# A two-layer decoder on one core: the context's conversion moved to GpSimd in halves, the odd heads' low parts to VectorE

## The reference, cut to what matters

```python
def _L0_xattn_ref(query, bank, Wq, bq, Wk, bk, Wv, bv, Wo, bo):
    q = split_heads(query @ Wq + bq)
    k = split_heads(bank @ Wk + bk)
    v = split_heads(bank @ Wv + bv)
    scores = jnp.einsum('bhqd,bhkd->bhqk', q, k) / scale
    attn = jax.nn.softmax(scores, axis=-1)
    out = jnp.einsum('bhqk,bhkd->bhqd', attn, v)
    ...
    return out @ Wo + bo
...
x = _layernorm(x + _L0_attn_ref(x, ...), axis=-1)
x = _layernorm(x + _L0_xattn_ref(x, ctx_1024, ...), axis=-1)
x = _layernorm(x + _L0_ffn_ref(x, ...), axis=-1)
x = _layernorm(x + _L1_attn_ref(x, ...), axis=-1)
x = _layernorm(x + _L1_xattn_ref(x, ctx_1024, mask_BxS2_ik0, ...), axis=-1)
x = _layernorm(x + _L1_ffn_ref(x, ...), axis=-1)
```

## Time and profile before

| | |
|---|---|
| median of 3 runs | 2411.67 us (2410.17 to 2414.68) |
| the profiled execution, its own time | 2410.11 us |
| its span, first to last instruction | 2408.3 us |
| mean granted clock of PE | 0.927 |
| busy: PE, PEld | 2155.8, 1981.5 us |
| busy: DVE, ACT, POOL | 1076.1, 961.1, 784.4 us |
| chain that ended last, by engine | PE 75%, DVE 9%, POOL 7%, issue 4%, ACT 4% |

### The profile page before, as it was taken

How to read it: one execution, slowest core, us unless ns; L and a number is a source line. 1 busy time by engine, 2 the same in 40 slices (tenths; PEclk the granted TensorE clock), 3 DMA queues, 4 the chain that set the end, 5 groups by cost and what they waited for, 6 DMA issues and landing times.

```text
span 2408.3 us, 36414 instructions
## 1 busy us (share of the span) xinstructions
PE 2155.8 (90%) x12528; PEld 1981.5 (82%) x12528; DVE 1076.1 (45%) x1728; ACT 961.1 (40%) x1623; POOL 784.4 (33%) x576
## 2 busy tenths in 40 slices
PE   4699999999765889689999999969999999999997
PEld 3688888888654778578888888869999999999987
DVE  8465666556456278435555666555510003000032
ACT  2255655455442244334555555442222223111132
POOL 4433332233333633422333323222222222222234
PEclk9799999999777978789999999979999999999999
DMA  4355455445321100254554545311112111111123
GB/s 152 119 136 141 131 143 152 117 131 139 106 65 31 38 8 0 80 176 126 136 141 133 143 133 156 110 54 61 61 62 61 61 53 61 61 61 61 61 70 98
DMA packets 127576, 230.56 MB, mean 96 GB/s; under 512 B 40024, under 2 KB 77144, under 8 KB 127384
## 3 DMA queue, kind: packets, MB, share of 16 engines
q1 hardware_dynamic: 127512, 229.71, 33.2%
HBM read 174.12 MB, written 55.53 MB: 95 GB/s over the span
## 4 chain that ended last, share of the span: by engine, by line
PE 75%; DVE 9%; POOL 7%; issue 4%; ACT 4%; DMA 1%; SPq 1%; POOLq 0%; DVEq 0%; ACTq 0%
PE psS L310 13%; PE psS L312 13%; PE psS L311 13%; PE psO L1638 5%; PE psJ L310 4%; PE psJ L311 4%; PE psJ L312 4%; PE psS L1595 3%; POOL cT_lo L511 3%; PE psT L310 2%; PE psT L311 2%; PE psT L312 2%; PE psT L1624 2%; PE psS L1624 2%; DVE psS L1162 1%
## 5 line engine op out<-in xcount | busy, mean ns | idle before, releaser
L703 POOL TENSOR_TENSOR fw_lo<-raw,fw_hi 128x1024 fp32r<-128x1024 f32 x96 | 235.1, 2451 | 551.4 <-ACT fw_hi L968 551.4
L310 PE MATMUL psS<-hid_hi,fw_hi 128*128 128x400 f32 x1152 | 398.2, 346 | 3.4 <-DVE hid_lo L1521 2.9
L312 PE MATMUL psS<-hid_hi,fw_lo 128*128 128x400 f32 x1152 | 399.0, 346 | 0.0
L311 PE MATMUL psS<-hid_lo,fw_hi 128*128 128x400 f32 x1152 | 398.6, 346 | 0.0
L518 POOL TENSOR_TENSOR pT<-p,pT 128x600 fp32r<-128x600 f32 x112 | 165.2, 1475 | 644.2 <-ACT pT L788 644.2
L1162 DVE TENSOR_REDUCE psS<-psS 100x1 f32<-100x722 f32 x256 | 234.7, 917 | 194.9 <-PE psS L1595 194.2
L1521 DVE TENSOR_TENSOR hid_lo<-h_act,hid_hi 128x800 fp32r<-128x800 f32 x32 | 40.8, 1343 | 528.1 <-ACT hid_hi L1057 528.1
L310 PE MATMUL psJ<-cT_hi,wk_hi 128*128 128x362 f32 (+1 forms) x512 | 190.2, 371 | 65.7 <-POOL cT_lo L511 39.2
L310 PEld LDWEIGHTS psS<-hid_hi,fw_hi 128*128 128x128 f32 x1152 | 217.3, 189 | 7.0 <-DVE hid_lo L1521 4.7
L312 PEld LDWEIGHTS psS<-hid_hi,fw_lo 128*128 128x128 f32 x1152 | 218.7, 190 | 0.0
L311 PEld LDWEIGHTS psS<-hid_lo,fw_hi 128*128 128x128 f32 x1152 | 217.2, 189 | 0.0
(11 more groups left out here) (318 smaller groups left out, 4573.7 us busy)
## 6 DMA issues: line engine op xcount, KB each, us to landing
kS<-k_parts SPq DMA_DIRECT2D x384, 180.5 KB
raw<-ffn_dram SPq DMA_DIRECT2D x96, 512.0 KB, 3.5
k_parts<-kst SPq DMA_DIRECT2D x64, 362.0 KB, 3.2
k_parts<-kst SPq DMA_DIRECT2D x64, 360.0 KB, 2.8
ctx_raw<-ctxT_dram SPq DMA_DIRECT2D x32, 361.0 KB, 3.9
ctx_late<-ctxT_dram SPq DMA_DIRECT2D x28, 361.0 KB, 3.8
qS<-q_parts SPq DMA_DIRECT2D x192, 50.0 KB, 2.2
q_parts<-qst SPq DMA_DIRECT2D x16, 400.0 KB, 2.5
```

The costliest lines, as they stand in the source:

```text
L310: nc.tensor.matmul(out, st[0], mv_[0], start=first, stop=False)
L311: nc.tensor.matmul(out, st[0], mv_[1], start=False, stop=False)
L312: return nc.tensor.matmul(out, st[1], mv_[0], start=False, stop=last)
L703: nc.gpsimd.tensor_tensor(fw.lo[:, e, :], raw[:, e, :], fw.hi[:, e, :], ALU.subtract)\
```

## The change

Four things are changed.

- The odd heads' plain exponential stays in PSUM for all pairs (psT), ahead of it the high part is written, and DVE makes the low part, at the end of each pair. POOL's `odd_probs_lo` and the tile p are gone. PE's waits for pT's high part or for POOL become waits for `att_lo_odd`, which DVE now raises.
- The context of the next batch is converted on POOL alone, high part (a `tensor_copy`, a CAST in the program) and low part, by halves of the keys: the first half of chunks 0 and 1 at pair 2, of chunks 2 and 3 at pair 3, the second half of all four at pair 4. The first half may be written after keys(3, 0), the last reader of it, and the second after keys(3, 1). SP loads chunks 2 and 3 by halves too. The stage's first batch is converted as before.
- keys of the next batch move one pair ahead: (0, 0), (0, 1), (1, 0), (1, 1) in the pairs 4, 5, 6, 7. keys(1, 1) leave the end of the batch. Only pair 3 is without keys, and has the rows set behind the odd exponentials.
- ACT applies the norm in pair 6 and not 3, POOL adds the bias in pair 6 and not 2. SP's order follows the keys.

The diff, cut to this:

```diff
-CONTEXT_AT = {2: (0,), 3: (1,), 4: (2, 3)}
-KEYLESS = (3, 4)
+KEYLESS = 3
 KEYS_AT = {0: (2, 1), 1: (3, 0), 2: (3, 1)}
-NEXT_KEYS_AT = {5: (0, 0), 6: (0, 1), 7: (1, 0)}
+NEXT_KEYS_AT = {4: (0, 0), 5: (0, 1), 6: (1, 0), 7: (1, 1)}
...
 SP
-            def context_rest(L, b):
-
-                wait_apart(sp, A.k_mm, 2 * C * (NB * L + b))
-                for c in range(2, C):
-                    sp.dma_start(ctx_late[:, c, :], d["ctxT"][c, :, bass.ds(b * KEYS, KEYS)])\
-                      .then_inc(A.more_in, 16)
+            def context_late(L, b, i):
+
+                k0, kn = HALVES[i]
+                wait_apart(sp, A.k_mm, 2 * C * (NB * L + b - 1) + 7 + i)
+                sp.dma_start(ctx_late[:, 2:4, k0:k0 + kn],
+                             d["ctxT"][2:4, :, bass.ds(b * KEYS + k0, kn)].rearrange("c p n -> p c n"))\
+                  .then_inc((A.late_a, A.late_b)[i], 16)
...
                     keys_out(L, b, 3, 0)
+                    if not last:
+                        context_late(L, b + 1, 0)
                     keys_in(L, b, 5)
                     if not last:
                         queries_in(L, b + 1, 0)
                     keys_out(L, b, 3, 1)
                     if not last:
-                        context_rest(L, b + 1)
+                        context_late(L, b + 1, 1)
...
 POOL
-            def odd_probs_lo(L, b, t):
-
-                h = 2 * t + 1
-                wait_apart(pool, A.pt_hi, H * (b + NB * L) + h + 1)
-                nc.gpsimd.tensor_tensor(pT[:, h % 4, :, T:2 * T], p[:, t % 2, :].rearrange("p (k t) -> p k t", k=NKC),
-                                        pT[:, h % 4, :, 0:T], ALU.subtract).then_inc(A.lo_odd, 1)
+            def context_half(L, b, cs, i):
+
+                n = b - 1 + (NB - 1) * L
+                for c in cs:
+                    if c < 2:
+                        wait_apart(pool, (A.ctx_in0, A.ctx_in1)[c], 16 * (b + NB * L + 1))
+                    else:
+                        wait_apart(pool, (A.late_a, A.late_b)[i], 16 * (n + 1))
+                    if c == 0:
+                        wait_apart(pool, A.k_mm, 2 * C * (b - 1 + NB * L) + 7 + i)
+                    src, hi, _ = half_part(c, i)
+                    nc.gpsimd.tensor_copy(hi, src).then_inc(A.half_hi, 1)
+                for c in cs:
+                    wait_apart(pool, A.half_hi, 8 * n + 4 * i + c + 1)
+                    src, hi, lo = half_part(c, i)
+                    nc.gpsimd.tensor_tensor(lo, src, hi, ALU.subtract).then_inc(A.half_lo, 1)
...
                     for t in range(PAIRS):
-                        if t != 4:
-                            odd_probs_lo(L, b, t)
...
-                        if t == 2:
+                        if t in (2, 3) and not last:
+                            context_half(L, b + 1, (2 * t - 4, 2 * t - 3), 0)
+                        if t == 4 and not last:
+                            context_half(L, b + 1, range(C), 1)
+                        if t == 6:
                             add_bias(L, b, None, base + b, A.resid_done)
-                        if t in CONTEXT_AT and not last:
-                            for c in CONTEXT_AT[t]:
-                                context_lo(L, b + 1, c)
...
 ACT
-                def odd_probs(b, t, psum=False):
+                def odd_probs(b, t):
 
                     B, h = b + NB * L, 2 * t + 1
-                    dst = st_view[1] if psum else p[:, t % 2, :].rearrange("p (i n) -> p i n", i=2)
                     act.wait_ge(A.st_mm, H * B + h + 1)
-                    wait(act, A.lo_odd, PAIRS * B + t - (0 if psum else 1))
...
+                    nc.scalar.activation(pT[:, h % 4, :, 0:T].rearrange("p (i k) t -> p i k t", i=2),
+                                         st_view[1].rearrange("p i (k t) -> p i k t", k=HK), ACT.Exp, scale=SCALE)\
+                      .then_inc(A.pt_hi, 1)
+                    nc.scalar.activation(st_view[1], st_view[1], ACT.Exp, scale=SCALE).then_inc(A.exped, 1)
...
-                        if t in KEYLESS and not last:
-                            context_hi(L, b + 1, CONTEXT_AT[t][0])
-                        if t < PAIRS - 1 and t not in KEYLESS:
+                        if t < PAIRS - 1 and t != KEYLESS:
                             max_rows(b, t + 1)
-                        odd_probs(b, t, psum=t == 4)
-                        if t in KEYLESS:
+                        odd_probs(b, t)
+                        if t == KEYLESS:
                             max_rows(b, t + 1)
-                        if t == 2 and not last:
-                            context_hi(L, b + 1, 0)
-                        if t == 3 and not first:
+                        if t == 6 and not first:
                             norm_apply(b - 1)
-                        if t == 4 and not last:
-                            context_hi(L, b + 1, 3)
...
 DVE
                         if t in NEXT_KEYS_AT and not last:
                             keys_lo(L, b + 1, *NEXT_KEYS_AT[t])
+                        low_parts(b, 2 * t + 1)
                         if t == 0 and not first:
                             norm_stats(base + b - 1, 0, y[:, 0, :])
-                        if t == 4:
-                            low_parts(b, 2 * t + 1)
...
 PE
-                if g == 0 and i == 0 and not weights and 0 in cs:
-                    pe.wait_ge(A.ctx_even, 2 * B + 2)
-                    pe.wait_ge(A.ctx_odd, 2 * B + 2)
                 for c in cs:
+                    if g == 0 and not weights and c in (0, 2):
+                        pe.wait_ge(A.half_lo, 8 * (b - 1 + (NB - 1) * L) + 4 * i + c + 2)
...
                     if h % 2 == 0:
                         wait(pe, A.lo_even, PAIRS * B + h // 2)
-                    elif h == 11:
-                        pe.wait_ge(A.lo_odd, PAIRS * B + 5)
                     else:
-                        wait(pe, A.pt_hi, H * B + h - 1)
+                        wait(pe, A.lo_odd, PAIRS * B + h // 2)
...
                     weighted(b, H - 1)
                     if not last:
-                        keys(L, b + 1, 1, 1)
                         scores(b + 1, 0)
```

More of the change, by code:

```diff
@@ L433, in attention_loads @@
                 first()
-                with nc.sync.Fori(0, NB - 1) as b:
+                batch(0, False)
+                with nc.sync.Fori(1, NB - 1) as b:
                     batch(b, False)
```

73 lines of the change are left out of this document (33 added, 40 removed).

## The result

The changed kernel takes 2517.5 us (median of 4 runs, 2514.8 to 2526.8), the kernel before 2412.0 (2410.2 to 2414.7) beside it: a ratio of 1.044, 95% interval 1.042 to 1.047. The forecast had the side right and the size wrong: it said 2455, +43, and +105 came. The profiled execution has a span of 2515.5 us and a mean granted clock of 0.905 (0.927 before). One run of all that follow, 2816.2 us at a granted clock of 0.71 in experiment 10, stands apart from the others of its kernel and is left out.

A forecast was written before the change was run, and what follows sets the result against it. TensorE, busy 90% of the span, was taken as the bound. The profiled 2410.1 us plus 31.5 for fourteen batches (+2.25 each, clock term included) and 13 for the last batches made 2454.6, forecast 2455, range 2412 to 2490.

The forecast's parts named there:

- The gain side: Savings a batch: context wait of 1.88 us gone, head 9 to 11 scores −0.4, 11 to 13 −1.5, keys(1, 1) −2.0.
- S11 to S13: On PE, from the start of head 11's scores to head 13's: 6.2 us in place of 7.72, −1.5.
- the slack: On GpSimd, idle time and 4 us before the converted context is wanted, said to cover the casts and subtractions.
- The ring: DVE's odd low part awaits ACT's exponential, delaying maximum and next odd scores: pairs with keys take 6.2 us, not 5.2.
- Rival B: The ring doesn't bind: pairs stay at PE's 5.2 us, 63.45 a batch, 2325 us, faster; chance 0.12.
- rival C: The context comes late and PE waits at keys(0, 1): 2 us in each of 14 batches, 2483 us; chance 0.06.
- 1.3 × 1.7 = 2.3: Clock term a batch: 1.3 stretches at 1.2 GHz after PE's waits, each costing 1.7 us.
- two longer ones, 5: Upper end of the clock term: two longer stretches at 1.2 GHz in a batch, 5 us.
- Rival A: The clock stays up: a batch takes 69.45 us, 2422 us in all; chance 0.22.
- +0.6 on the 68.85: Sum of all interval changes in a batch at full clock, on the 68.85 us batch read before: 69.45.
- keys(1, 1) leave the end of the batch: −2.0: On PE behind head 15's scores: twelve projection matmuls go, 2.0 us less; the pair after keeps its length.
- +6.5 a stage, 13 in all: Each stage's last batch, keyless from pair 3: +1.6 for two intervals, +4.0 up to head 9's scores, −0.7 at the end.

The follow-up runs named there:

- experiment 10: The kernel before, context and keys untouched, with all odd low parts on DVE behind the next pair's even maximum and the fold of the outputs: 2458.4 us.
- experiment 7: The changed kernel, its DVE order untouched, with eleven unused 128x362 matmuls in pair 3 and eleven more in pair 1: 2456.6 us.
- Experiment 1: The changed kernel with DVE's odd low part moved behind the next even head's maximum, still ahead of the fold of the outputs: 2397.0 us.
- experiment 5: The changed kernel with DVE's odd low part moved behind both the next even head's maximum and the fold of the outputs: 2374.9 us.
- experiment 9: experiment 6 with six more unused matmuls in each of the pairs 3 to 6 of both last batches: 2344.7 us.
- experiment 11: experiment 4 with GpSimd converting the context ahead of the odd low part in pairs 2 to 4, no filler: 2333.1 us.
- experiment 4: The changed kernel with the odd heads' low parts back on GpSimd in all pairs, ahead of the context's conversion: 2480.7 us.
- experiment 6: experiment 5 with six unused 128x362 matmuls added in pair 3: 2352.8 us.
- experiment 12: experiment 11 with the unused matmuls of experiment 9: 2335.7 us.

## Why the prediction was right or wrong

**The gain side held.** The 1.88 wait for the context is gone, and S11 to S13 fell by 1.6 in experiment 7 (forecast −1.5), S9 to S11 by 0.38 (forecast −0.4). The casts (0.49) were within the bounds, the subtractions took 0.97 and not 0.87, and the slack covered both.

**The ring held.** Intervals measured without the clock's part, in experiment 7: S2 to S5 +1.6 (forecast +1.7), S5 to S7 +0.95 (+0.9), S7 to S9 +1.6 (+1.4), S13 to S15 +0.7 (+0.5). Rival B is out, and so is rival C: no wait for the context's low part is among those of stage 0. Experiment 1 is the direct proof: with the low part elsewhere 120 of the changed kernel's 2517 us go, the stretches at 1.2 GHz that hung on the ring among them.

**Three terms were mis-sized**, and they make up the 62 us between 2455 and 2517.5.

*The clock, "1.3 × 1.7 = 2.3" a batch.* This is the step that failed most. Measured: 76.03 less the 71.46 of experiment 7, both means over fourteen, 4.57 a batch, 2.27 × 14 = 32 us more. I had the number of stretches about right (1.3 a batch, and the trace has 20 in fourteen), and took the cost of one, 1.7 us, from one batch of the kernel before. In the changed kernel a stretch mostly lasts about 10 us, and such a one costs 4.1 us (75.2 against the 71.1 of experiment 7; 4.4 in experiment 5), about two and a half times what I gave it. The kernel before already had such stretches, in batches that I didn't read; here is one of four, and then the one that I read:

```profile
188.79:259.34 70.55, 66.96 (x421) 59.19 (x420) 42.07 (x71) 38.10 (x68) 21.41 (x19) 0.93 0.50 135
...
328.35:397.21 68.86, 64.27 (x422) 56.86 (x420) 42.07 (x71) 38.10 (x68) 21.43 (x19) 0.98 0.51 138
```

My upper bound, "two longer ones, 5", held it. Rival A, the clock stays up, is out; had it come, it would not have been 2422 either, but near the 2456.6 of experiment 7. The Trainium skill (TensorE: Matmul & The Clock Gate, HAM oscillation) blames, in that section, idle gaps longer than any in these batches; by it the clock term would be 0. The traces disagree: waits of 1.8 to 2.0 us at a sparse pair were followed by 1.2 GHz again and again, and filling the pairs took 61 us off (2517.5 to 2456.6).

*The ring's full clock sum, "+0.6 on the 68.85".* It was 71.1, another 1.65 × 14 = 23 us. Most of that is "keys(1, 1) leave the end of the batch: −2.0", which came as −0.7. I wrote that the pair after S15 keeps its length, and did not look at what queues behind the odd low part of pair 6. It is the fold, and `weighted` waits for it: 0.74 in the rows above. Experiments 1 and 5 show it: 16.0 with the low part ahead of the fold, 14.45 with the fold ahead. I had looked for what is queued behind the waiting instruction and found the maximum, but not the fold. The rest is 0.2 in each of two rounds, and that is the fold too. It stands behind the even maximum, ends at 388.34 (387.78 + 0.56 above), and `weighted` starts at 388.49; so from S15 to the turned maxima it takes 2.76 and not 2.48. Behind S5, where no fold is due, it took 2.53 even after a wait of 1.98.

*The last batches, "+6.5 a stage, 13 in all".* Measured +6 and +15. In stage 0 the figure is about right. In stage 1 S2 to S15 takes 42.9 us where it took 29.4, +13.5, and behind S15 it is +1.7. Up to S9 it is +4.3, as forecast (+4.0). From S9 to S15, windows of the kernel before and of the changed one:

```profile
1563.66:1576.42 12.76, 10.93 (x91) 9.38 (x91) 10.61 (x20) 8.95 (x17) 4.05 (x4) 1.00 0.43 107
```

```profile
1659.98:1681.87 21.89, 19.30 (x91) 16.76 (x91) 12.12 (x22) 8.37 (x15) 0.00 (x0) 0.50 0.22 52
```

These are three intervals, and I had counted two, +1.6 each. They took 6.4, 7.8 and 7.8 us at 1.2 GHz, where my ring had 5.9. So one interval was left out, and the clock was given no term here. Filling the last pairs gained 8 us in experiment 9, but in a kernel with another ring, so how the 9.1 us divide between ring and clock is not shown.

32 + 23 + 8 = 63 us, against 62.5. That the sum closes is no proof, since the last batches are what the fourteen left over.

**What the forecast did not see at all** is that the change was two changes of opposite sign, large ones. It summed them into "+0.6 a batch" and called the side by the clock. The side would have been right without the clock, for a reason that I had not summed so: with the gaps filled (experiment 7) the changed kernel is still 44 us slower, by the ring and the fold. The half with the context was worth −79 us by itself, close to what rival B worked out (63.45 a batch and 2325; experiment 11, with the odd low parts still on GpSimd, has 63.8 and 2333). I had tied that gain to the condition that the ring doesn't bind, and read the 12% as small; the ring did bind, but only for where one line stands, and with that line moved (experiment 5) a batch at full clock takes 64.4.

## What to carry to other kernels

Moving work to an engine with room is judged by what stands behind it in that engine's queue, and by when its input comes, before its duration is: a 0.78 us instruction that waits for late data cost 143 us more at the end of a pair than two places later, and the same fault on GpSimd (experiment 4 against 11) cost 148; both numbers hold the clock's part. For each such instruction list everything behind it that another engine waits for, not only the nearest; the fold was missed that way, in the prediction and in experiment 1. And when a change has parts that can stand alone, time them alone, each in its best place, before judging the whole.

## What the runs showed of the hardware

A short wait on TensorE can cost more than its length, by the lower clock behind it. In the changed kernel every one of the fourteen waits of about 1.8 us ahead of S9, in the pair without keys, went with a stretch at 0.50, mostly of some 10 us. Ahead of S5 the same wait of 1.98 us left the clock at 1.00 in the first of the two batches shown and was followed by such a stretch in the second. In experiment 5 waits of 0.54 and 0.59 us within 2 us stood where it began, and the same two in the batches that stayed at full clock; experiment 11 has the 0.54 there and not the 0.59, and no stretch. A stretch of 10 us costs 4.1 us in the changed kernel and 4.4 in experiment 5, so that unused matmuls in the gap pay: −40 us for 11 in pair 3, a further −21 for 11 in pair 1, −22 for six in experiment 6, −11 in the kernel before, and nothing where the clock was up already (experiment 12). In stage 0 of experiment 5 batches with equal instructions alternate between 64.4 and 68.8 us; what decides which of the two a batch becomes was not found.

On GpSimd a cast from fp32 to fp32r of 128x362 takes 490 ns and a subtraction of that shape 0.96 to 0.97 us, against 1.72 for 128x722.
